# Cross-attention tails as alternating 64x32 tiles, and a new order at the seam to the next stage

## The chip, the cores and the metric

The kernel is one program on one NeuronCore of a Trainium2 chip. The metric is the device time of one execution in microseconds, as the median of a few runs. TensorE is called PE in the profile, and PEld its weight loads; VectorE is DVE, ScalarE ACT, GpSimd POOL, and SyncE (SP) issues most of the DMAs.

## The reference

The input x is 16 batches of 64 rows of 512. Three residual blocks follow, each on a layer norm of x: a cross-attention to 1601 context rows of 256, a causal-masked self-attention (16 query heads, 4 key heads), and a mixture of 8 experts with the best two chosen for each row. The change is in the cross-attention and in the first instructions of the self-attention. The core of the cross-attention, with 16 heads of 32:

```python
y_dca, y_main = y[:, -16:, :], y[:, :-16, :]        # 16 and 1585 rows
q = _ln(heads(x @ Wq + bq))
k, v = _ln(heads(y_main @ Wk + bk)), heads(y_main @ Wv + bv)
k_dca, v_dca = _ln(heads(kv_dca[..., 0])), heads(kv_dca[..., 1])   # from y_dca @ Wkv_dca
ctx = softmax(q k^T * SCALE) v + softmax(q k_dca^T * SCALE) v_dca
out = ctx @ Wo + bo
```

So each query has two softmaxes: one over 1585 main keys and one over 16 second keys. Their weighted values are each divided by their own sum, and then added.

## The kernel before, in words

**Tiles.** The 1585 main rows of a batch are CH = 13 chunks of 128 rows; the last one (column LAST = 12, the "tail") has only LM = 49 rows. A turn of the loop handles two batches, and their chunks are "units" 0 to 25. The tails of the two batches are projected together, in one chunk. A chunk is projected by TensorE to keys and values (split_product, L106, in float32r parts), the keys are normalised per head and transposed (L87), and `scores` (L1300) multiplies them with the queries in 64x128 tiles (L1327). ScalarE takes the exponential into `probs` (L1035), with keys on partitions and 16 heads x 64 queries in the columns. `weighted` (L1331) multiplies values and probs: for each head the stationary operand is 128 rows by 32 columns, the moving operand 64 columns, and the output goes to one of four column tiles (32 partitions of PSUM each), in bank O_BANK. VectorE adds up the probs of the units 0 to 11 in `total` (L1197), for the sum below the fraction.

**The tail.** In the tail's probs buffer the 49 main keys and the 16 second keys lie in different halves of the 128 partitions: `TAIL_ROWS, DCA_ROWS = (0, 64), (DCA_ROW, 0)`, with DCA_ROW = 64. So for the first batch of a pair the main keys are on partitions 0 to 48 and the second ones on 64 to 79, for the second batch the other way round. `g.v_last[:, half, n]` holds the values on all 128 partitions, for n = 0 the main ones and for n = 1 the second ones, each with zeros in the other half. `weighted` makes 16 calls for n = 0 into O_BANK and 16 for n = 1 into V_BANK, all over 128 rows. `counts` (L1355) adds the sums of the probs: four calls of 256 columns a time, with the stationary `g.counted` that is 1 on the rows that count. It is called for n = 1, for n = 0, and at last with `total`, for which it first waits for VectorE (semaphore `pa`). An f32 matmul call stands as two records of LDWEIGHTS and two of MATMUL in the trace.

**Order.** Everything is an order written out by hand for each engine, with semaphores between them. The units come in twelve groups a turn, the last of each batch with three units, (10, 11, 12) and (23, 24, 25). In a group TensorE does the projections of the second group ahead, the transposes of the next, then the weighted values of this group's units and the scores of the next one's. Before unit 11 it waits for `ex` and `ve` of unit 11, and before the tail for `ex` of the tail, `ve` of the latest projected chunk (its values pass through V_BANK, which the tail overwrites) and `vd`, the DMA of the second values. After the tail ScalarE copies both banks to `o_sb` (`o_evac`, L1038), and the next batch's projected values wait for that. The last pair of batches has no next one; there `first_product` and `first_rows` already form the output rows of the first two tiles of the next stage, and `first_seed`, `first_norm` their layer norm. `first_seed(1)` (L1064, ScalarE) stands behind the last `o_evac`.

**The seam.** The cross-attention and the self-attention are two blocks with a barrier between them. Each engine starts the self-attention with a list of increments that sets its semaphores to their first values (L1763, L1842, L1976). TensorE's first work is `turn_x(0, 0)` (L1996), transposes that wait for `xn` (VectorE's list) and `cte` (ScalarE's); ScalarE then evacuates them as xT, and `turn_x(0, 1)` waits for that. The q products follow (L2013). VectorE starts with the normalisation of batch 15's cross-attention (L1847 to L1852), GpSimd splits the weights wo (L1752).

Of the kernel before, what the change touches and what calls it, by code (L numbers as in the profile page):

```python
# [22 lines left out]
B, SQ, D = 16, 64, 512  # L23
# [4 lines left out]
KD = D // P  # L28
# [717 lines left out]
def cross_attention(nc, io, g, psum):  # L746
# [3 lines left out]
    with ExitStack() as ctx:  # L750
# [36 lines left out]
        def unit(i, u):  # L787

            i, u = at(i, u, UNITS)
            return i * UNITS + (UNITS + u + 1)  # L790
# [9 lines left out]
        def tail(n):  # L800

            return column(n) == LAST
# [93 lines left out]
        with nc.Block() as block:  # L896
# [69 lines left out]
            def _(act):  # L966
# [102 lines left out]
                def steps(i, room, guarded):  # L1069
                    for group in range(GR):  # L1070
# [7 lines left out]
                        for j in range(3):  # L1078
# [7 lines left out]
                            if j == len(project) - 1:  # L1086
                                seeds(i, project)
                        if group in (5, 11):
                            o_evac(i * 2 + group // 6, i, GROUP[group][-1])
                        if not room and group == GR - 1:  # L1090
                            first_seed(1)

# [180 lines left out]
            def _(pe):  # L1273
# [57 lines left out]
                def weighted(i, u, latest):  # L1331
                    half = u // CH
                    pe.wait_ge(s["ex"], unit(i, u))
                    pe.wait_ge(s["ve"], projected(i, latest if tail(u) else u))
                    if column(u) == 0:
                        pe.wait_ge(s["oe"], i * 2 + (half + 1))
                    if tail(u):
                        pe.wait_ge(s[f"vd{half}"], i * 16 + 16)
                    for n in range(2 if tail(u) else 1):
                        bank = V_BANK if n else O_BANK  # L1340
                        for k in range(KD):
                            for r in range(4):
                                h = k // 2 * 8 + r * 2 + k % 2
                                v = g.v_last[:, half, n, h, :] if tail(u) else g.v[:, (u - half) % VBUFS, h, :]
                                last = pe.matmul(psum[r * HD:(r + 1) * HD, bank, k * SQ:(k + 1) * SQ], v,  # L1345
                                                 probs[:, buf(u), place(h) * SQ:(place(h) + 1) * SQ],
                                                 start=(k == 0 and (column(u) == 0 or n == 1)), stop=tail(u), skip_group_check=True)
                    if tail(u):
                        for n, bank in ((1, V_BANK), (0, O_BANK)):
                            last = counts(bank, g.counted[:, half * 2 + n], probs[:, buf(u), :], n == 1)  # L1350
                        pe.wait_ge(s["pa"], added(i, u - 1))
                        last = counts(O_BANK, g.counted[:, 4], total[:], True)
                    last.then_inc(s["pv"], 1)

                def counts(bank, rows, src, stop):  # L1355
# [320 lines left out]
def self_attention(nc, io, g, psum):  # L1676
# [6 lines left out]
    with ExitStack() as ctx:  # L1683
# [35 lines left out]
        with nc.Block() as block:  # L1719
# [42 lines left out]
            def _(act):  # L1762
                for stage in ("xe", "qe", "ve", "ex", "pe0", "pe1", "cte"):  # L1763
                    act.sem_inc(s[stage], 2)
# [75 lines left out]
            @block.vector  # L1840
            def _(dve):
                for stage in ("ke", "sm", "mx", "sb", "ri", "co", "x2"):  # L1842
                    dve.sem_inc(s[stage], 2)
                for stage in ("tp", "x1", "bs", "ba", "rn1", "rn2", "rs", "xn"):
                    dve.sem_inc(s[stage], 4)

# [128 lines left out]
            def _(pe):  # L1975
                for stage in ("trx", "qp", "kp", "vp", "sp", "pt0", "pt1", "pv", "trc", "op2"):  # L1976
                    pe.sem_inc(s[stage], 2)
                pe.sem_inc(s["op"], 4)

# [109 lines left out]

                turn_x(0, 0)  # L2090
                turn_x(0, 1)

# [495 lines left out]
```

## Time and profile before

| | us |
|---|---|
| median of 3 runs (1406.8 to 1413.03) | 1407.89 |
| the profiled execution's own time | 1407.75 |
| its span, from the first to the last instruction | 1405.9 |

Busy over the span, from the page:

```profile
PE 1314.5 (93%) x16104; PEld 1078.5 (77%) x16104; DVE 990.8 (70%) x1811; ACT 850.2 (60%) x1535; POOL 311.7 (22%) x354
PE   6889999999999999999999999999999799965896
PEclk9989999999999999999999999999999999986999
```

The first line has each engine's busy us, its share and the number of its instructions. The two others cut the span in 40 slices of 35 us: the busy tenths of TensorE, and its granted clock in tenths of 2.4 GHz. The cross-attention fills the slices 3 to 31, the self-attention follows, and the experts come last. The trace's matmuls are pipelined and overlap, so the sum of their times over a stretch says less than the distance from one start to the next.

### The profile page before, as it was taken

The numbers are of one execution on the slowest core, as the hardware profiler recorded it, in microseconds if no ns is written. First come the engines' busy times: TensorE is split into PE (matmuls) and PEld (weight loads), VectorE is DVE, ScalarE is ACT, GpSimd is POOL, SyncE is SP. The second block draws the span as 40 slices with busy tenths as digits, with TensorE's granted clock in tenths as the row PEclk, the third lists the DMA queues.
The fourth block names the chain that finished last, engine by engine and source line by source line (L and its number), as shares of the span: only waits on it lengthen the run. The fifth ranks groups of instructions, "written<-read, shape, count | busy, mean of one in ns | idle before, by whom it ended". The sixth has DMA issues, their size and how long they took to land. (4 is left out here: it accounts for less than half of the span.)

```text
span 1405.9 us, 42510 instructions
## 1 busy us (share of the span) xinstructions
PE 1314.5 (93%) x16104; PEld 1078.5 (77%) x16104; DVE 990.8 (70%) x1811; ACT 850.2 (60%) x1535; POOL 311.7 (22%) x354
## 2 busy tenths in 40 slices
PE   6889999999999999999999999999999799965896
PEld 3468888888888888888888888888877677744785
DVE  7847677776767776776767777776867656665764
ACT  2346776766777676767766767667666333334653
POOL 2312121221212121221212121221211302111465
PEclk9989999999999999999999999999999999986999
DMA  7042110210210120111112110210200100016887
GB/s 267 16 163 75 47 33 17 96 33 17 70 53 24 32 96 17 33 47 66 33 32 78 36 33 17 97 33 17 75 21 2 65 1 32 31 47 211 210 189 136
DMA packets 35098, 91.26 MB, mean 65 GB/s; under 512 B 4039, under 2 KB 7626, under 8 KB 33418
## 3 DMA queue, kind: packets, MB, share of 16 engines
q1 hardware_dynamic: 28064, 72.38, 15.5%
q0 software_dynamic: 6432, 16.32, 5.2%
q8 instruction: 135, 2.21, 0.7%
q14 instruction: 33, 0.27, 0.1%
q10 hardware_dynamic: 434, 0.08, 0.0%
HBM read 71.93 MB, written 36.01 MB: 77 GB/s over the span
## 5 line engine op out<-in xcount | busy, mean ns | idle before, releaser
L1105 POOL TENSOR_TENSOR y_lo<-y_sb,y_hi 128x256 fp32r<-128x256 f32 x190 | 143.1, 753 | 803.1 <-ACT y_hi L984 803.1
L1018 ACT ACTIVATE ksq<-kc 128x512 f32<-128x512 f32 x200 | 126.4, 632 | 230.0 <-DVE kc L1142 226.4
L1142 DVE TENSOR_TENSOR kc<-psum,bk_sb 128x512 f32<-128x512 f32 x200 | 137.6, 688 | 142.4 <-PE psum L106 139.8
L1035 ACT ACTIVATE probs<-psum 128x1024 f32<-128x1024 f32 x208 | 201.0, 1023 | 39.0 <-PE psum L1327 37.7
L1327 PE MATMUL psum<-qbd,k 64*128 64x128 f32 x3328 | 211.9, 278 | 0.1
L1327 PEld LDWEIGHTS psum<-qbd,k 64*128 64x128 f32 x3328 | 193.3, 188 | 14.0 <-issue 6.3
L1197 DVE TENSOR_TENSOR total<-total,probs 128x1024 f32<-128x1024 f32 x160 | 194.1, 1213 | 1.4 <-ACT probs L1035 1.2
L106 PE MATMUL psum<-wk_hi,y_hi 128*128 128x512 f32 x400 | 177.3, 443 | 11.5 <-issue 8.3
L1148 DVE TENSOR_REDUCE kss<-ksq 128x16 f32<-128x512 f32 x200 | 134.1, 670 | 46.2 <-ACT ksq L1018 45.9
L106 PE MATMUL psum<-wv_hi,y_hi 128*128 128x512 f32 x400 | 157.5, 394 | 2.4 <-ACT v_sb L1011 2.4
L997 ACT ACTIVATE k<-psum,cols_sb 128x512 f32<-128x512 f32 x192 | 150.7, 785 | 13.9 <-PE psum L87 13.9
L106 PE MATMUL psum<-wk_hi,y_lo 128*128 128x512 f32 x400 | 157.7, 394 | 0.0
L106 PE MATMUL psum<-wv_hi,y_lo 128*128 128x512 f32 x400 | 157.1, 393 | 0.0
L106 PE MATMUL psum<-wk_lo,y_hi 128*128 128x512 f32 x400 | 156.8, 392 | 0.0
L106 PE MATMUL psum<-wv_lo,y_hi 128*128 128x512 f32 x400 | 156.3, 391 | 0.0
L1166 DVE SCALAR_TENSOR_TENSOR kn<-kc,kr 128x1024 f32<-128x1024 f32 x96 | 125.8, 1311 | 8.7
L87 PE MATMUL psum<-ident_sb,kn 128*128 128x128 f32 x800 | 120.2, 273 | 3.2 <-DVE kn L1166 3.1
L87 PEld LDWEIGHTS psum<-ident_sb,kn 128*128 128x128 f32 x800 | 98.0, 139 | 32.4 <-DVE kn L1166 7.3
L1011 ACT COPY v_sb<-psum 128x512 f32<-128x512 f32 x192 | 112.3, 585 | 3.6 <-PE psum L106 0.3
L1345 PE MATMUL psum<-probs,v_sb 128*32 128x64 f32 x6144 | 105.7, 220 | 0.0
L1345 PEld LDWEIGHTS psum<-probs,v_sb 128*32 128x32 f32 x6144 | 90.2, 110 | 18.3 <-issue 18.3
L106 PEld LDWEIGHTS psum<-wk_hi,y_hi 128*128 128x128 f32 x400 | 75.5, 189 | 33.7 <-issue 13.6
(272 smaller groups left out, 2033.5 us busy)
## 6 DMA issues: line engine op xcount, KB each, us to landing
y_sb<-in_y SPq DMA_DIRECT2D x48, 512.0 KB, 3.6
slots_dram<-in_blank SPq DMA_DIRECT2D x9, 2080.0 KB
expert_raw<-in_experts SPq DMA_DIRECT2D x8, 1024.0 KB, 6.8
x_sb<-slots_dram SPq DMA_DIRECT2D x23, 260.0 KB, 3.1
x_sb<-in_x SPq DMA_DIRECT2D x1, 1536.0 KB, 10.2
wq<-in_wq SPq DMA_DIRECT2D x4, 256.0 KB, 4.3
xa_wo<-in_wo SPq DMA_DIRECT2D x1, 1024.0 KB, 12.1
y_tail<-in_y_tail SPq DMA_DIRECT2D x8, 128.0 KB, 22.0
```

What stands on the lines that cost most here:

```text
L87: last = pe.transpose(bank[:, k * P:(k + 1) * P], src[:, k * P:(k + 1) * P], ident)
L106: last = pe.matmul(bank, lhs, rhs, start=(n == 0), stop=(n == len(todo) - 1))
L997: last = nc.scalar.activation(k32[:, buf(n)], bank, ACT.Identity, scale=g.cols[:, 2:3], bias=g.cols[:, 3:4])
L1018: nc.scalar.activation(sq[:, buf(n)], kc[:, buf(n)], ACT.Square).then_inc(s["ksq"], 1)
L1035: nc.scalar.activation(probs[:, buf(u), :], psum[:, bank:bank + 2, :].rearrange("p a n -> p (a n)"), ACT.Exp, scale=SCALE).then_inc(s["ex" ...
L1105: nc.gpsimd.tensor_tensor(g.y_lo[:, buf(n)], src, g.y_hi[:, buf(n)].bitcast(F32), ALU.subtract).then_inc(s["ylo"], 1)
L1142: nc.vector.tensor_tensor(kc[:, buf(n)], psum[:, K_BANK, :], g.bk[:], ALU.add).then_inc(s["kb"], 1)
L1148: nc.vector.tensor_reduce(ss[:, buf(n)], head_view(sq[:, buf(n)]), AX_X, ALU.add).then_inc(s["krd"], 1)
L1166: nc.vector.scalar_tensor_tensor(out=kn[:, 0:m].rearrange("p m (h d) -> p (m h) d", d=HD), in0=kc[:, 0:m].rearrange("p m (h d) -> p (m h) ...
L1197: nc.vector.tensor_tensor(total[:], total[:], probs[:, buf(u), :], ALU.add).then_inc(s["pa"], 1)
L1327: last = pe.matmul(out[n][a], k32[rows, k_buf(u), n, :], g.qbd[rows, n, :], start=not guarded, stop=True, skip_group_check=True)
L1345: last = pe.matmul(psum[r * HD:(r + 1) * HD, bank, k * SQ:(k + 1) * SQ], v, probs[:, buf(u), place(h) * SQ:(place(h) + 1) * SQ], start=(k ...
```

## The change

Three things change.

1. The tail. `weighted` sends the tail to a new `weighted_tail`. It makes the same 32 calls for the values and 8 for the counts, but over 64 rows each: those of the main keys and those of the second keys in turn, n = 0 and n = 1 after one another for each head. All values come first, then the counts of both; the total's sums stand behind them, as before over 128 rows. The three waits of the tail move ahead of unit 11 (`tail_ready`).
2. The end of the cross-attention. In the last group ScalarE does `first_seed(1)` before the last `o_evac`.
3. The start of the self-attention. ScalarE's and VectorE's lists of increments begin with those that the first transposes wait for; TensorE gives two of its eleven increments before `turn_x(0, 0)` and nine between `turn_x(0, 0)` and `turn_x(0, 1)`.

```diff
@@ ScalarE, cross-attention, end of a group
+                        if not room and group == GR - 1:
+                            first_seed(1)
                         if group in (5, 11):
                             o_evac(i * 2 + group // 6, i, GROUP[group][-1])
-                        if not room and group == GR - 1:
-                            first_seed(1)
@@ TensorE, cross-attention
                 def weighted(i, u, latest):
                     half = u // CH
-                    pe.wait_ge(s["ex"], unit(i, u))
-                    pe.wait_ge(s["ve"], projected(i, latest if tail(u) else u))
+                    if column(u) == LAST - 1:
+                        tail_ready(i, u + 1, latest)
+                    elif not tail(u):
+                        pe.wait_ge(s["ex"], unit(i, u))
+                        pe.wait_ge(s["ve"], projected(i, u))
                     if column(u) == 0:
                         pe.wait_ge(s["oe"], i * 2 + (half + 1))
                     if tail(u):
-                        pe.wait_ge(s[f"vd{half}"], i * 16 + 16)
...
+                        weighted_tail(u, half)
+                        pe.wait_ge(s["pa"], added(i, u - 1))
+                        last = counts(O_BANK, g.counted[:, 4], total[:], True)
+                    else:
...
+                def tail_ready(i, u, latest):
+                    pe.wait_ge(s["ex"], unit(i, u))
+                    pe.wait_ge(s["ve"], projected(i, latest))
+                    pe.wait_ge(s[f"vd{u // CH}"], i * 16 + 16)
+
+                def weighted_tail(u, half):
+                    parts = [(n, slice(first, first + SQ), (O_BANK, V_BANK)[n])
+                             for n, first in enumerate((TAIL_ROWS[half], DCA_ROWS[half]))]
+                    for k in range(KD):
+                        for r in range(4):
+                            h = k // 2 * 8 + r * 2 + k % 2
+                            for n, rows, bank in parts:
+                                pe.matmul(psum[r * HD:(r + 1) * HD, bank, k * SQ:(k + 1) * SQ], g.v_last[rows, half, n, h, :],
+                                          probs[rows, 2, place(h) * SQ:(place(h) + 1) * SQ],
+                                          start=(k == 0 and n == 1), stop=True, skip_group_check=True)
+                    for r in range(4):
+                        for n, rows, bank in parts:
+                            pe.matmul(psum[r * HD:(r + 1) * HD, bank, KD * SQ:2 * KD * SQ], g.counted[rows, half * 2 + n],
+                                      heads_in(probs[rows, 2, :], r), start=False, stop=(n == 1), skip_group_check=True)
@@ ScalarE, self-attention
-                for stage in ("xe", "qe", "ve", "ex", "pe0", "pe1", "cte"):
+                for stage in ("cte", "xe", "pe0", "pe1", "qe", "ve", "ex"):
@@ VectorE, self-attention
+                for stage in ("xn", "tp", "x1", "bs", "ba", "rn1", "rn2", "rs"):
+                    dve.sem_inc(s[stage], 4)
                 for stage in ("ke", "sm", "mx", "sb", "ri", "co", "x2"):
                     dve.sem_inc(s[stage], 2)
-                for stage in ("tp", "x1", "bs", "ba", "rn1", "rn2", "rs", "xn"):
-                    dve.sem_inc(s[stage], 4)
@@ TensorE, self-attention
-                for stage in ("trx", "qp", "kp", "vp", "sp", "pt0", "pt1", "pv", "trc", "op2"):
+                for stage in ("vp", "trx"):
                     pe.sem_inc(s[stage], 2)
-                pe.sem_inc(s["op"], 4)
...
                 turn_x(0, 0)
+                for stage in ("qp", "kp", "sp", "pt0", "pt1", "pv", "trc", "op2"):
+                    pe.sem_inc(s[stage], 2)
+                pe.sem_inc(s["op"], 4)
                 turn_x(0, 1)
```

## Rows read from the trace of the kernel before

**Rows 1.** Stretches: length, busy PE, PEld, DVE, ACT, POOL; clock, DMA share, GB/s.

```profile
109.80:1090.00 980.20, 971.81 (x13694) 812.45 (x13692) 717.23 (x1072) 680.55 (x1207) 190.93 (x239) 1.00 0.13 44
1098.00:1102.00 4.00, 0.00 (x0) 0.00 (x0) 1.02 (x4) 0.64 (x3) 1.13 (x2) 1.00 0.03 5
1102.00:1108.00 6.00, 4.43 (x20) 4.09 (x21) 5.63 (x3) 2.87 (x3) 2.80 (x5) 0.51 0.96 335
1231.80:1235.00 3.20, 1.19 (x34) 0.92 (x33) 3.17 (x5) 1.06 (x1) 0.00 (x0) 1.00 0.02 5
1235.20:1238.50 3.30, 3.30 (x38) 2.97 (x39) 3.16 (x11) 1.85 (x3) 0.00 (x0) 0.50 0.00 0
```

**Rows 2.** Timeline, PE, first tail: start, us, line, what, tile, count.

```profile
153.56 0.60 PE L87 MATMUL psum<-ident_sb,kn 128*128 128x128 f32 x4
154.09 1.10 PE L1345 MATMUL psum<-probs,v_sb 128*32 128x64 f32 x64
155.01 1.08 PE L1345 MATMUL psum<-probs,v_last 128*32 128x64 f32 x64
155.90 1.05 PE L1358 MATMUL psum<-probs,counted 128*32 128x256 f32 x16
156.76 0.61 PE L1358 MATMUL psum<-total,counted 128*32 128x256 f32 x8
157.31 1.94 PE L1327 MATMUL psum<-qbd,k 64*128 64x128 f32 x30
```

**Rows 3.** Timeline, PE, shorter stretches: the last transpose, the last four sum records.

```profile
153.89 0.27 PE L87 MATMUL psum<-ident_sb,kn 128*128 128x128 f32 x1
...
156.98 0.40 PE L1358 MATMUL psum<-total,counted 128*32 128x256 f32 x4
```

**Rows 4.** Timeline, PE, self-attention scores in 64x64 tiles.

```profile
1153.87 1.10 PE L2038 MATMUL psum<-sa_kT,sa_qT 64*64 64x128 f32 x32
```

**Rows 5.** Timeline, weight loads in flight from 154.08 to 154.14 us.

```profile
154.09 0.16 PEld L1345 LDWEIGHTS psum<-probs,v_sb 128*32 128x32 f32 x8 [0.17 <-issue]
```

**Rows 6.** One line's instructions: ns shortest/median/longest, starts, tile.

```profile
L1345 PEld LDWEIGHTS psum<-probs,v_sb x6144: 106/110/110, 100.9 to 1094.6; 128*32 128x32 f32 x199
L1327 PE MATMUL psum<-qbd,k x3328: 272/272/373, 92.0 to 1090.0; 64*128 64x128 f32 x196
```

**Rows 7.** Timeline, ACT and DVE beside the first tail; brackets: idle before, releaser.

```profile
153.76 0.59 ACT L1011 COPY v_sb<-psum 128x512 f32<-128x512 f32 x1
...
154.37 1.21 DVE L1197 TENSOR_TENSOR total<-total,probs 128x1024 f32<-128x1024 f32 x1
...
157.44 1.07 ACT L1043 COPY o_sb<-psum 128x512 f32<-128x512 f32 x2 [1.58 <-PE psum L1358]
```

**Rows 8.** Timeline, ACT and DVE, end of the cross-attention.

```profile
1096.10 0.18 DVE L1243 BATCH_NORM_AGGREGATE sa_mv<-sa_st 128x2 f32<-128x6 f32 x1
1097.17 1.07 ACT L1043 COPY o_sb<-psum 128x512 f32<-128x512 f32 x2 [5.39 <-PE psum L1358]
...
1098.47 0.20 ACT L114 ACTIVATE sa_rseed<-sa_rlog 128x1 f32<-128x1 f32 x1
...
1099.29 0.55 DVE L1250 TENSOR_SCALAR kc<-x_sb,sa_mv,sa_rs 128x512 f32<-128x512 f32 x1
```

**Rows 9.** One line's instructions: the increments of TensorE and VectorE after the barrier.

```profile
L1977 PEldq EVENT_SEMAPHORE  x10: 51/51/51, 1100.9 to 1102.4; - x10
...
L1845 DVEq EVENT_SEMAPHORE  x8: 21/21/21, 1101.5 to 1102.2; - x8
```

**Rows 10.** Timeline, PE, DVE and POOL, start of the self-attention.

```profile
1102.80 1.09 PE L87 MATMUL psum<-ident_sb,kc 128*128 128x128 f32 x4 [5.70 <-DVEq L1845]
1104.66 1.09 PE L87 MATMUL psum<-ident_sb,kc 128*128 128x128 f32 x4 [0.77 <-ACT sa_xT L1778]
...
1106.39 4.53 POOL L1752 TENSOR_TENSOR wo_lo<-xa_wo,wo_hi 128x2048 fp32r<-128x2048 f32 x1 [2.96 <-ACT wo_hi L1811]
1106.41 4.78 DVE L1852 TENSOR_TENSOR ctxT<-o_sb 128x256 f32<-128x256 f32 x1
```

More of the change, by code:

```diff
@@ L1337, in weighted @@
                     if tail(u):
-                        pe.wait_ge(s[f"vd{half}"], i * 16 + 16)
-                    for n in range(2 if tail(u) else 1):
-                        bank = V_BANK if n else O_BANK
+                        weighted_tail(u, half)
+                        pe.wait_ge(s["pa"], added(i, u - 1))
+                        last = counts(O_BANK, g.counted[:, 4], total[:], True)
+                    else:
                         for k in range(KD):
@@ L1343, in weighted @@
                                 h = k // 2 * 8 + r * 2 + k % 2
-                                v = g.v_last[:, half, n, h, :] if tail(u) else g.v[:, (u - half) % VBUFS, h, :]
-                                last = pe.matmul(psum[r * HD:(r + 1) * HD, bank, k * SQ:(k + 1) * SQ], v,
+                                last = pe.matmul(psum[r * HD:(r + 1) * HD, O_BANK, k * SQ:(k + 1) * SQ],
+                                                 g.v[:, (u - half) % VBUFS, h, :],
                                                  probs[:, buf(u), place(h) * SQ:(place(h) + 1) * SQ],
-                                                 start=(k == 0 and (column(u) == 0 or n == 1)), stop=tail(u), skip_group_check=True)
@@ L1348, in weighted @@
[L1348 to L1352, printed above, removed]
-                    last.then_inc(s["pv"], 1)
+                                                 start=(k == 0 and column(u) == 0), stop=False, skip_group_check=True)
```

## The prediction

> **What bounds the kernel now.** I read the table of stretches first, then one batch's tail in order of time, then the seam between the two stages. In the cross-attention loop TensorE is nearly the only limit: from 109.8 to 1090 us it is busy 971.81 of 980.20 us at the full clock, VectorE 717 and ScalarE 681 [rows 1]. What TensorE stops needing there leaves the span almost whole. At the seam it is another chain: TensorE is idle for 5.70 us up to 1102.80 [rows 10], and small work of ScalarE and VectorE, a barrier and a list of increments set the time.
>
> **A tail today.** Units 10 and 11 are 64 records from 154.09 to 155.01, the tail's v_last products 64 records to 155.90 (0.89 us), its counts 16 records to 156.76 (0.86), the total's sums 8 records to 157.31 (0.55); then come scores [rows 2]. An f32 call leaves two records (32 calls, 64 records): 14 ns a record in the products and 54 in the counts. Alone, a 256-column record would need about 0.22 us: a 128-column transpose holds the array 0.11 us (four last 0.60, the last one 0.27 of it [rows 2, 3]), and the second four sum records start 0.22 us after the first four (156.76 and 156.98 [rows 2, 3]). So the four column tiles already run side by side and the array streams without gaps.
>
> **The new tail.** The same 40 calls use 64 rows each, the batch's own values on one half of the rows and the second values on the other. Eight tiles can be in flight instead of four. Does one row half run beside the other? The self-attention scores are 64x64 tiles, two by two: 32 records of 128 columns in 1.10 us [rows 4]; less the last one's 0.27, as 128 columns last [rows 6], that is 0.12 us for each four, the time of one. The loads keep up there. Eight at once are shown nowhere. They need a load and a matmul every 7 ns; after a change of shape eight loads are issued within 0.16 - 0.11 = 0.05 us [rows 5, 6] (0.11 is one load), 7 ns each, which just suffices: 64 x 7 ns = 0.45 us. Half of the present times is 0.445 for v_last and 0.43 for the counts. Gross gain 0.875 us; the bounds are 0 (the halves take turns) and 0.875.
>
> **Two more changes of shape.** A tail went from 128x128 to 128x32 and then to 64x128. Now 128x32 to 64x32 and back come in between. A new shape starts 0.07 us before the modelled end of the last old matmul: 153.89 + 0.27 against 154.09, and 156.98 + 0.40 against 157.31 [rows 2, 3]. Without a change the next group would have started 0.11 and 0.22 us after the last: the changes cost 0.09 and 0.11, the second also a slow first group (373 against 272 ns [rows 6]), 0.21 in all. For the new ones: into 64x32, a 64-column matmul lasts 0.22, so 0.15 after its start less the 0.04 in which the next would have come, 0.11; back, 0.14, since the last eight starts are spread over 0.05; 0.04 for slower first groups. I take 0.29, nearer to the first row because 32 columns are loaded as there; bounds 2 x 0.09 and 2 x 0.21. Net per tail 0.875 - 0.29 = 0.58 us, bounds -0.42 and +0.70.
>
> The Trainium skill speaks against small tiles: TensorEngine Tiling (Array Packing), Instruction Overhead, gives each matmul some 60 cycles, whatever its columns. At 2.4 GHz that is an estimate of 25 ns; 80 records would take 2.0 us against 1.75 now, and a tail would lose. The trace disagrees, with 14 ns a record [rows 2]: such a cost, if there is one, overlaps between tiles.
>
> **The waits moved ahead of unit 11 (LAST - 1).** There TensorE now asks for the tail's exponentials, the latest values' evacuation and the second values. The evacuation is the late one: it ends at 153.76 + 0.59 = 154.35 [rows 7], 0.26 after unit 10 began, and unit 11 is due 0.46 after. Unit 10 hides it; without that cover it would be up to 0.1 us a tail. Behind the wait in TensorE's queue stand unit 11 and the tail, for which ScalarE's o_sb copies wait. The sums need VectorE's last addition, which ends at 154.37 + 1.21 = 155.58 [rows 7]; they would now start near 156.2: no new wait. The o_sb copies wait for TensorE alone (ScalarE idle 1.58 before them [rows 7]) and move with it, as do the next exponentials. Nothing else closes up, so 15 tails give 15 x 0.58 = 8.7 us. The sixteenth does not count: the seam hides it.
>
> **The seam, its end.** ScalarE copies batch 15's sums from 1097.17 for 1.07 us and only then forms the seed for which VectorE was ready at 1096.10 + 0.18 = 1096.28. The seed is there at 1098.67, VectorE ends at 1099.84, 1.17 later [rows 8]. With the seed first, it is there at about 1096.90 (I allow 0.6) and VectorE ends at 1098.07. TensorE is done near 1096.5, the copies run from 1096.93 to 1098.00; moving them behind the seed delays them by 0.4 us that nobody needs. Both ends come together near 1098.07: 1.77 us earlier.
>
> **The seam, its start.** TensorE's increments begin at 1100.9, 0.1 after the barrier, ten of them to 1102.4 and one more, 0.16 us each; VectorE's last (xn) comes at 1102.2 [rows 9], and the first transposes start at 1102.80 [rows 10], 2.0 after the barrier. Now two increments and a wait stand ahead of them, and xn and cte are first in their lists: 0.6. What is late next is TensorE's own queue: nine increments (1.45 us) ahead of turn_x(0, 1), which starts some 2.5 after the barrier, where before it waited for xT until 1104.66, 3.9 after [rows 10]. The q products gain 1.6, with the transposes still at the full clock. VectorE's list is only reordered and its reciprocal keeps its place; but its ctxT step was held for 4.78 us from 1106.41 beside GpSimd's wo_lo (1106.39, 4.53 us) [rows 10], and wo_lo follows xT and wo_hi, so it comes earlier by as much. Bounds of this step: 0 (VectorE sets the pace) and 1.9 (2.0 - 0.6, and twice half of a 1.09 us group). The loads on SP's queue start 1.8 us earlier and nothing here waits for them.
>
> The clock is 1.00 (2.4 GHz) up to 1102 and 0.51 (nearly all at 1.2 GHz) from 1102 to 1108, after 4 us without a matmul [rows 1]. The new idle is 3.1 us, then 0.5 us of transposes, then 1.3 us idle. A stretch with 1.19 of 3.2 us busy was followed by 0.50, too [rows 1], so I expect the fall again. Between 1105.5 and 1108 or a little more it hit dense work, some 3.4 us, of which half is lost. Where it ends may shift by as much again: I take -0.75 us, bounds +1.7 (no fall) and -1.7. Seam: 1.77 + 1.6 - 0.75 = 2.6 us, bounds 0.1 and 5.4.
>
> **The sum.** 8.7 + 2.6 = 11.3. The profiled execution took 1407.75 us (span 1405.9 and 1.85 around it), 0.14 under the median, 1407.89. 1407.89 - 11.3 = 1396.6; I say 1396.5.
>
> **Rivals.**
> (a) The loads of the two row halves take turns. v_last keeps 0.89 and only the counts halve: 0.43 - 0.29 = 0.14 a tail, 2.1 + 2.6 = 4.7 in all, 1403.2. For it: loads come 14 ns apart now, and eight tiles are new. Against it: the 64x64 tiles [rows 4]. The Trainium skill has a rule near it: TensorE: Matmul & The Clock Gate, "Step-by-step: what each phase is for", lets a load's time go with its columns and not with its rows; by itself it says only that no load gets shorter.
> (b) The other side: no more than four matmuls stream at once, whatever the tiles. Both packed shapes of the trace show four and never more [rows 2, 4]. Nothing is won in a tail and the changes of shape are paid: 15 x 0.29 to 15 x 0.42 = 4.4 to 6.3 us, less the seam's 2.6: 1409.7 to 1411.6. It decides from the point where the eight-tile part of a tail, now 1.75 us, takes 1.75 + 0.17 - 0.29 = 1.63 or more (15 x 0.17 is the seam's gain). Against it: halves by rows run as freely there as tiles by columns.
> (c) VectorE's reciprocal and the held ctxT step set the first keys' copies whatever TensorE does: 1.77 remains, less the clock's 0.75: 9.7 in all, 1398.2.
> (d) The clock does not fall at the seam: +1.7 instead of -0.75, 13.8 in all, 1394.1. For it the shorter idle, against it the half-busy stretch.
>
> **Chances.** Forecast 0.50, (c) 0.18, (d) 0.10, (a) 0.11, (b) 0.07, tails at half their gain 0.04. A measurement of this kernel tells about 0.5%, 7 us, from no change: the line is 1400.9. Forecast, (c), (d) and half of the mixed case lie below it: faster 0.80. (a), the rest of that case and part of (b) lie within: 0.16. Slower by over 7 us needs the upper end of (b) and a lost seam: 0.04. The range, 1393.5 to 1403.5, takes in (d), (c) and (a).
>
> **What would show it.** In a tail: v_last's 64 records in 0.45 us and the counts' 16 in 0.43, the sums 2.1 us after unit 10's start instead of 2.67, scores 2.6 after it instead of 3.22. v_last still at 0.89 means (a) or (b), counts at 0.86 (b). At the seam: seed ahead of the copies, transposes 0.6 us after the barrier, the second ones behind nine increments. The forecast fails if the loop outside the tails grows by what the tails give, as it would if another engine paced it.

## The result and the profile after

The changed kernel takes 1400.21 us, the median of 6 runs (1399.86 to 1401.78), against 1408.18 for the kernel before (6 runs, 1406.8 to 1413.03). The ratio is 0.9938, interval 0.9925 to 0.9952. The forecast was 1396.5: right in direction, inside its range, 3.7 us too low. The profiled execution took 1399.86 us with a span of 1398.0, 7.9 less than the span before.

Busy over the span, and the granted clock, from the page after:

```profile
PE 1308.3 (94%) x16104; PEld 1069.2 (76%) x16104; DVE 990.8 (71%) x1811; ACT 851.0 (61%) x1535; POOL 312.4 (22%) x354
...
PEclk9989999999999999999999999999999999976998
```

The first tail on TensorE (timeline: start, us, line, what, tile, count), answering to [rows 2]:

```profile
154.55 1.10 PE L1348 MATMUL psum<-probs,v_sb 128*32 128x64 f32 x64
155.58 0.80 PE L1368 MATMUL psum<-probs,v_last 64*32 64x64 f32 x60
156.16 0.40 PE L1373 MATMUL psum<-probs,counted 64*32 64x256 f32 x1
156.18 0.22 PE L1368 MATMUL psum<-probs,v_last 64*32 64x64 f32 x1
156.18 0.40 PE L1373 MATMUL psum<-probs,counted 64*32 64x256 f32 x1
156.19 0.25 PE L1368 MATMUL psum<-probs,v_last 64*32 64x64 f32 x3
156.24 0.70 PE L1373 MATMUL psum<-probs,counted 64*32 64x256 f32 x14
156.87 0.64 PE L1379 MATMUL psum<-total,counted 128*32 128x256 f32 x8
157.44 2.06 PE L1327 MATMUL psum<-qbd,k 64*128 64x128 f32 x32
```

From unit 10's start, before and after: the tail's values at +0.92 and +1.03, the counts at +1.81 and +1.61, the total's sums at +2.67 and +2.32, the scores at +3.22 and +2.89. So a tail gained 0.33 us. Twelve of the fifteen tails that count are within 0.03 us of +2.89; three are later, by 1.4 us together. In the kernel before two of the fifteen are, by 1.7 together: stalls that stay.

The same timeline, cut off at two points after the values' first start, shows how many had begun, here x32 within 0.265 us and x33 within 0.275:

```profile
155.58 0.46 PE L1368 MATMUL psum<-probs,v_last 64*32 64x64 f32 x32
...
155.58 0.48 PE L1368 MATMUL psum<-probs,v_last 64*32 64x64 f32 x33
```

In fact 32 had begun within 0.24 us, and the 64th began at 0.642.

The end of the cross-attention, ScalarE and VectorE, answering to [rows 8]:

```profile
1092.41 0.30 ACT L112 ACTIVATE sa_rlog<-sa_mv,cols_sb 128x1 f32<-128x1 f32 x1 [4.53 <-DVE sa_mv L1243]
1092.74 0.20 ACT L114 ACTIVATE sa_rseed<-sa_rlog 128x1 f32<-128x1 f32 x1
1092.93 1.07 ACT L1043 COPY o_sb<-psum 128x512 f32<-128x512 f32 x2
...
1093.56 0.55 DVE L1250 TENSOR_SCALAR kc<-x_sb,sa_mv,sa_rs 128x512 f32<-128x512 f32 x1
```

The start of the self-attention on TensorE, then VectorE and GpSimd, answering to [rows 10]:

```profile
1089.91 1.10 PE L1348 MATMUL psum<-probs,v_sb 128*32 128x64 f32 x64
...
1095.63 0.63 PE L87 MATMUL psum<-ident_sb,kc 128*128 128x128 f32 x4 [2.76 <-DVEq L1864]
1097.21 0.92 PE L87 MATMUL psum<-ident_sb,kc 128*128 128x128 f32 x4 [0.95 <-ACT sa_xT L1799]
1097.92 5.12 PE L2033 MATMUL psum<-sa_xT,sa_wq 128*128 128x128 f32 x32
...
1110.12 1.10 PE L2058 MATMUL psum<-sa_kT,sa_qT 64*64 64x128 f32 x32
```

```profile
1098.76 4.53 POOL L1773 TENSOR_TENSOR wo_lo<-xa_wo,wo_hi 128x2048 fp32r<-128x2048 f32 x1 [1.05 <-ACT wo_hi L1832]
1099.96 3.87 DVE L1870 TENSOR_TENSOR o_sb<-o_sb 128x512 f32<-128x512 f32 x1
```

And stretches there (columns as in [rows 1]), first of the kernel before, then after:

```profile
1102.10:1108.85 6.75, 5.28 (x24) 4.94 (x25) 6.48 (x3) 2.87 (x3) 3.55 (x5) 0.50 0.92 327
```

```profile
1097.42:1100.80 3.38, 3.38 (x18) 3.38 (x17) 3.35 (x2) 1.74 (x2) 2.27 (x3) 0.50 0.91 335
1100.84:1110.00 9.16, 9.16 (x84) 9.15 (x82) 6.56 (x10) 2.22 (x6) 6.61 (x5) 1.00 0.24 98
```

Counted from unit 10 of the last batch (1093.82 before, 1089.91 after), the first transposes come at +8.99 and +5.71, the q products at +11.72 and +8.01, the first scores at +24.14 and +20.20. The 7.9 us of the span are: the loop from its first weighted values (unit 0) to the last unit 10, 992.88 to 988.50, 4.38; the seam up to the scores 3.94; 0.05 after them; and 0.47 lost ahead of the loop, which began later (unit 0's values at 101.41, not 100.94). That last part varies from one profiled kernel to the next, between 100.2 and 103.2.

### The profile page after: what moved, and what is told of

The parts are those of the page before. It is cut to its first block and busy times, and to the rows that moved or that the text cites. A ratio compares the mean times of both kernels' runs of the same rounds, so it can differ in the third digit from the quotient of the medians.

```text
span 1398.0 us, 42494 instructions
## 1 busy us (share of the span) xinstructions
PE 1308.3 (94%) x16104; PEld 1069.2 (76%) x16104; DVE 990.8 (71%) x1811; ACT 851.0 (61%) x1535; POOL 312.4 (22%) x354
## 6 DMA issues: line engine op xcount, KB each, us to landing
xa_wo<-in_wo SPq DMA_DIRECT2D x1, 1024.0 KB, 12.1
```

## The experiments

Ten other kernels and the changed one once more ran in three groups, each group with the kernel before on the same chip (medians 1407.24, 1408.08, 1406.88). The ratios are those on record, to the kernel before of the same group; they are not the quotients of the two medians and differ from them by up to 0.0007.

### The two halves of the change

Tail alone: the changed kernel with the seam as it was.

```diff
-                        if not room and group == GR - 1:
-                            first_seed(1)
                         if group in (5, 11):
                             o_evac(i * 2 + group // 6, i, GROUP[group][-1])
+                        if not room and group == GR - 1:
+                            first_seed(1)
...                      and the three lists of increments as before
```

> The change without its seam (order of the seed and of the three lists of increments as before). By the trace of the changed kernel a tail's scores start 2.89 us after unit 10 instead of 3.22: 15 x 0.33 = 5.0 us. Theory S (the two parts are independent and both real): 1408.2 - 5.0 = 1403.2 us, ratio near 0.9965, the seam from unit 10 of the last batch to the first q products 11.4 us, as before. Rival: the seam's gain is what moves everything and the tails' gain is used up elsewhere: under 2 us of gain here.

Measured: 1404.05 us (9 runs), ratio 0.997, 0.9957 to 0.9983. The tails are as in the changed kernel, scores at +2.89 (two are late); the seam as before less the sixteenth tail's gain: scores +23.76.

Seam alone: the kernel before with the two other parts of the change (the inverse edit).

> Only the seam of the change, tails as before. Theory S: 3 to 4 us less than before, 1404.5 us, since from unit 10 of the last batch to the first q products it is 8.0 us instead of 11.7 in the changed kernel (0.3 of this is the tail's). Rival: most of this is the clock's phase (3.4 us at 1.2 GHz in the changed kernel's profile, 6.8 before) and the median moves by 2 us at most.

Measured: 1403.26 us (10 runs), ratio 0.9974, 0.9964 to 0.9983. First transposes +5.81, q products +7.77, scores +20.21: 3.93 us less than before. The two halves are worth 3.2 and 4.0 us by the medians, 7.2 together; the whole change 8.0 beside its own runs of before, and 6.2 when it was run again (below). So they add up as far as the times can tell. By the intervals the tails give 2.4 to 6.1 us and the seam 2.4 to 5.1, so the seam is worth about as much as the tails, where the forecast had 2.6 against 8.7.

### Why a tail gave 0.33 us and not 0.58

The next kernels change only the order or the size of the tail's calls. Two theories had to explain the break after 32 records. "Supply": the loads and matmuls that TensorE has at hand run out after 32 pairs and refill at a slower pace. "Places in flight": only 32 pairs of load and matmul can be under way, so the 33rd waits until the first is done. The forecast's rival (a) said that loads of the two halves take turns.

Halves in turn: all calls of one row half, then all of the other.

```diff
-                    for k in range(KD):
-                        for r in range(4):
-                            h = k // 2 * 8 + r * 2 + k % 2
-                            for n, rows, bank in parts:
+                    for n, rows, bank in parts:
+                        for k in range(KD):
+                            for r in range(4):
+                                h = k // 2 * 8 + r * 2 + k % 2
...                      the counts likewise, but the other half first
```

> The changed kernel, but the 64-row tiles of one row half all come before those of the other half, values and counts, so that no more than four tiles can stream at once; the two changes of shape stay. It prices the changes of shape alone. Theory P: products 0.89 us and counts 0.86 as before the change, plus 0.29 for the changes of shape: scores 3.5 us after unit 10, 0.6 later than in the changed kernel, 15 x 0.6 = 9 us over it, about 1409 us. Rival: the changes of shape are dearer than 0.29, which would explain why a tail won only 0.33 instead of 0.58: then scores come at 3.75 or later, 1413 us.

```profile
154.53 0.96 PE L1368 MATMUL psum<-probs,v_last 64*32 64x64 f32 x62
155.27 0.38 PE L1373 MATMUL psum<-probs,counted 64*32 64x256 f32 x1
155.29 0.23 PE L1368 MATMUL psum<-probs,v_last 64*32 64x64 f32 x2
155.37 0.66 PE L1373 MATMUL psum<-probs,counted 64*32 64x256 f32 x15
155.96 0.64 PE L1379 MATMUL psum<-total,counted 128*32 128x256 f32 x8
156.53 1.94 PE L1327 MATMUL psum<-qbd,k 64*128 64x128 f32 x29
```

Measured: 1401.87 us (5 runs), ratio 0.9965, 0.9952 to 0.9978; scores at +2.98 in most tails (+3.04 in the one shown), only 0.09 us behind the alternating order. My expectation of 0.6 us a tail failed. The program has all values ahead of all counts, yet a count starts (155.27) before the last two values (155.29): TensorE starts matmuls of different tiles out of the program's order. In the changed kernel the rows at 156.16 and 156.18 show the same. It also finds work for the idle half by itself: in the second tail the starts come in fours, some 56 ns apart, up to 0.267 us, as with four tiles, and from 0.274 on others stand between them. The record does not name the half; that these are the second one's, whose first call is the 33rd, is read from that pattern. The Trainium skill (TensorE: Matmul & The Clock Gate, "The mechanism") has matmuls start and end strictly in the program's order, with only loads pulled ahead; for the starts the rows at 155.27 and 155.29 disagree, and the measurement decides.

Counts between: the 8 calls of the counts after the first half of the values.

```diff
-                    for r in range(4):
-                        for n, rows, bank in parts:
...
+                        if k == 1:
+                            for r in range(4):
+                                for n, rows, bank in parts:
+                                    pe.matmul(...                      the counts' call, unchanged
```

> The changed kernel, but the eight count calls stand between the first and the second half of the value calls. In the changed kernel the first 28 value records of a tail start 7 ns apart and the rest 8.4 ns apart with two gaps of 0.03 and 0.06 us. Theory Q (supply): TensorE's queue holds a store of prepared instructions, and once it is empty they come only every 8.4 ns a pair; while the counts stream (0.43 us for 16 records) the queue fills again, so that the second half of the values runs at 7 ns, too: values to sums 1.05 us instead of 1.29, 0.24 less a tail, 3.6 us in all, about 1396.6 us. Rival theory R (the array): eight tiles of 64 columns can't keep 7 ns for long, since loads of a row half and matmuls of the same half get into each other's way; then the second half takes as long as now and the time stays within 1 us of the changed kernel's.

```profile
154.59 0.45 PE L1368 MATMUL psum<-probs,v_last 64*32 64x64 f32 x32
154.85 0.78 PE L1374 MATMUL psum<-probs,counted 64*32 64x256 f32 x16
155.28 0.81 PE L1368 MATMUL psum<-probs,v_last 64*32 64x64 f32 x32
156.02 0.64 PE L1380 MATMUL psum<-total,counted 128*32 128x256 f32 x8
156.59 2.06 PE L1327 MATMUL psum<-qbd,k 64*128 64x128 f32 x32
```

Measured: 1399.89 us (5 runs), ratio 0.9945, 0.9932 to 0.9958. The sums start at +2.32 and the scores at +2.89, as in the changed kernel (the tail shown is 0.15 us late). The counts gave the time in which a supply could refill, yet in the second tail the second half of the values took 0.44 us for 32 records, 14 ns each and not 7: "supply" falls. The 33rd record is now a count, and starts 0.26 us after the first (154.85 against 154.59): the break stands at the place in the queue, whatever the work.

Narrow values: the tail's value products stream 16 columns instead of 64 (the output lacks 48 of 64 queries in that part).

```diff
-                                pe.matmul(psum[r * HD:(r + 1) * HD, bank, k * SQ:(k + 1) * SQ], g.v_last[rows, half, n, h, :],
-                                          probs[rows, 2, place(h) * SQ:(place(h) + 1) * SQ],
+                                pe.matmul(psum[r * HD:(r + 1) * HD, bank, k * SQ:k * SQ + 16], g.v_last[rows, half, n, h, :],
+                                          probs[rows, 2, place(h) * SQ:place(h) * SQ + 16],
```

> The changed kernel with 16 instead of 64 columns in the tail's value calls; the tail's values for the other 48 queries of each batch are left out. One look at the pace. In the changed kernel the 33rd value record of every tail starts 0.267 us after the first and the 64th 0.642 us after it. Theory F (in flight): TensorE holds at most 32 load-and-matmul pairs, so the 33rd can only start when the first is done; a record with 16 columns is done 0.04 us sooner, so the 33rd starts near 0.227 and the last near 0.54. Rival Q' (supply): pairs are handed out every 8.4 ns whatever they do: 0.267 and 0.642 stay. Rival R (the array's eight tiles can't stream 64 columns at 7 ns): only the columns bind, and with a quarter of them the records run at 7 ns throughout: last at 0.44.

The timeline again, cut off 0.22 and 0.235 us after the first start:

```profile
154.40 0.35 PE L1368 MATMUL psum<-probs,v_last 64*32 64x16 f32 x32
...
154.40 0.40 PE L1368 MATMUL psum<-probs,v_last 64*32 64x16 f32 x33
```

Measured: 1398.93 us (one run); the 33rd record starts 0.227 us after the first, not 0.267. In the tail of the changed kernel one record of 256 columns lasts 0.40 us and one of 64 columns 0.22, so 48 columns are worth 0.18 x 48 / 192 = 0.045 us, and the break ends earlier by about that. In both kernels the 33rd starts 0.027 us behind the modelled end of the first record (0.240 and 0.200 us). So the break ends when the first pair is done: "places in flight" is borne out for it, 32 pairs, that is 64 instructions. The Trainium skill (TensorE: Matmul & The Clock Gate, "The mechanism") gives TensorE a 64-deep window; the trace agrees. What comes behind the break stays open. The 64th value starts at 0.551 us here (expected 0.54) and at 0.642 in the changed kernel: 10.4 and 12.1 ns a record on the average. In the changed kernel the 34th starts 0.056 us behind the 33rd, the next ones 16.7 ns apart up to 0.41, as if only one half had work, and from there both halves together start a record each 8.4 ns; this last pace is the same with 16 columns. 32 places of 0.24 us each would allow one each 7.5 ns, so full places alone do not explain it.

Sums first: the total's sums ahead of the tail, with VectorE's last addition one step earlier, so that the values follow the sums and not unit 11.

```diff
                     if tail(u):
-                        weighted_tail(u, half)
                         pe.wait_ge(s["pa"], added(i, u - 1))
-                        last = counts(O_BANK, g.counted[:, 4], total[:], True)
+                        counts(O_BANK, g.counted[:, 4], total[:], False)
+                        last = weighted_tail(u, half)
```

> The changed kernel, but the total's sums stand before the tail (still 128x32, behind unit 11) and not behind it, so that the tail's 64x32 is followed by the scores' 64x128 at once: one change of shape less in a tail. To have the total ready, VectorE adds unit 11 right after the first k_reduce of that group instead of after the second. Theory: a change back costs 0.14 to 0.16 us, so scores come 0.15 sooner, 2.74 after unit 10, 15 x 0.15 = 2.3 us below the changed kernel, near 1398 us. Rival: the sums' 256-column records leave 0.4 us each in flight, so the tail's first ones start later, and the projection that VectorE now serves 0.4 us later delays TensorE: no gain or a loss.

```profile
155.08 0.62 PE L1382 MATMUL psum<-total,counted 128*32 128x256 f32 x8
155.63 0.80 PE L1370 MATMUL psum<-probs,v_last 64*32 64x64 f32 x60
...
156.92 1.83 PE L1329 MATMUL psum<-qbd,k 64*128 64x128 f32 x28
```

Measured: 1400.24 us (5 runs), ratio 0.9949, 0.9937 to 0.9962: no gain over the changed kernel. The scores start 2.76 us after unit 10 (154.16), 0.13 earlier, 1.9 us over 15 tails. But at the seam the slow clock lasted 6.8 us and the first scores there came at +20.74 instead of +20.20, in the loop of the profiled execution the clock fell once for 3.4 us, and its late tails cost 2.3 us, not 1.4. Whether one change of shape less is worth its 0.13 us in the time is therefore not shown. The 33rd value started 0.267 us after the first here too.

Counts alone: only the 8 count calls use the halves, the values stay over 128 rows, first all of the main keys and then all of the second.

```diff
-                                pe.matmul(psum[...], g.v_last[rows, half, n, h, :],
-                                          probs[rows, 2, ...
+                                pe.matmul(psum[...], g.v_last[:, half, n, h, :],
+                                          probs[:, 2, ...
```

> The changed kernel with the tail's 32 value calls back over all 128 rows (first those of the main keys, then those of the second keys); only the 8 calls for the counts use 64 rows in alternating halves. Theory (places in flight): in the changed kernel the counts, with the change of shape behind them, took 0.71 us (2.32 - 1.61) where they took 0.86 before, and the values with the change ahead of them 1.61 - 0.11 less than before: nearly all of a tail's gain is in the values' first 32 records. Values alone in four tiles keep 0.89 us, the change of shape now stands ahead of the counts: counts at +1.9 us after unit 10's start, sums at +2.6, scores at +3.2, so 0.0 to 0.1 us a tail are gained over before, and with the seam's 4.0 the time is 1403 to 1404. Prediction's sizing (counts halve to 0.43, two changes cost 0.29): counts +1.92, sums +2.49, scores +3.08, 0.14 us a tail, 1402. Scores later than +3.3 would mean that the change of shape costs more than the counts give.

```profile
157.26 1.08 PE L1368 MATMUL psum<-probs,v_last 128*32 128x64 f32 x64
158.26 0.66 PE L1373 MATMUL psum<-probs,counted 64*32 64x256 f32 x16
158.85 0.64 PE L1379 MATMUL psum<-total,counted 128*32 128x256 f32 x8
159.42 1.04 PE L1327 MATMUL psum<-qbd,k 64*128 64x128 f32 x13
```

Measured: 1404.15 us (12 runs), ratio 0.9975, 0.9966 to 0.9984. From unit 10's start (156.34) the counts come at +1.92, the sums at +2.51, the scores at +3.09: 0.13 us gained a tail. The time does not confirm it: with the seam's 4.0 and 15 x 0.13 it should be 6 us under the kernel before, and it is 2.7 by the medians. The profile has the first unit 10 2.2 us later than that of before and the low clock in the loop once, so that its loop is no shorter (939.7 us from the first tail's unit 10 to the last's in both). Over all its executions the granted clock is not lower than that of before (0.976 in both), so the rest is open. The prediction's sizing of counts and shape changes, 0.43 - 0.29 = 0.14, is what was measured, and the theory that I set against it (0.0 to 0.1) had it too low; both readings are of the trace. So of the 0.33 us the values gave 0.20, where the forecast had 0.445.

### The seam

Seed first alone, in the kernel before:

```diff
+                        if not room and group == GR - 1:
+                            first_seed(1)
                         if group in (5, 11):
                             o_evac(i * 2 + group // 6, i, GROUP[group][-1])
-                        if not room and group == GR - 1:
-                            first_seed(1)
```

> The kernel before with one edit: the last seed ahead of the last o_sb copies. Theory: VectorE's last instruction and the barrier come 1.4 to 1.8 us sooner, so about 1.6 us less, ratio 0.9989. Rival: the copies, pushed back by the seed, end the block, so under 1 us is won.

```profile
1100.08 0.63 PE L87 MATMUL psum<-ident_sb,kc 128*128 128x128 f32 x4 [3.79 <-DVEq L1845]
1101.47 1.09 PE L87 MATMUL psum<-ident_sb,kc 128*128 128x128 f32 x4 [0.77 <-ACT sa_xT L1778]
```

Measured: 1406.52 us (11 runs), ratio 0.9991, 0.9981 to 1.0. From unit 10 of the last batch (1093.00) the first transposes come at +7.08, 1.91 earlier than before; the q products at +9.35, 2.37 earlier, as the first transposes now run at the full clock (0.63 us, not 1.09); the scores at +21.15, 2.99 earlier. The slow clock lasted 3.4 us. In the time this is 1.6 us by the medians, as expected, and the interval reaches to no gain: the 2.99 us of the one trace are not confirmed by it.

Increments alone, in the kernel before (the third part of the change as the diff ahead shows it):

> The kernel before with the new order of the three lists of increments only. Theory: first transposes 0.6 instead of 2.0 us after the barrier, q products 1.6 to 2 us sooner, 2 us less, ratio 0.9986, and 3.4 us at 1.2 GHz at the seam instead of 6.8, as in the four kernels with both parts. Rival: the shorter slow stretch needs both parts (the shorter idle), and here it stays 6.8: 1.3 us less.

```profile
1104.27 1.09 PE L87 MATMUL psum<-ident_sb,kc 128*128 128x128 f32 x4 [4.25 <-DVEq L1843]
```

Measured: 1409.66 us (the median of 12 runs, one of which took 3254.89 us and is not in the ratio; its cause is not known), ratio 1.0005, 0.9996 to 1.0014: no gain, where 2 us were expected. In the trace the first transposes come at +7.54 (1.45 earlier), the q products at +10.28 (1.44), the scores at +22.33 (1.81 earlier). But unit 10 of the last batch came at 1096.73, 2.9 us later than before: 1.3 before the first unit 10, and 1.6 in the loop, where the clock was once low for 3.4 us near 1028. Such a fall is worth 1.7 us, an estimate: half of its 3.4. Of the twelve profiles beside that of before, six have it and six have not, but near there, in the last turn, TensorE is idle in all thirteen, fall or not: it waits 2.1 to 2.4 us for ScalarE's copy of the values. The other executions have no profile, only a granted clock: 0.9743 on the average of eleven, against 0.9753 for the 23 of the kernel before. That is an estimate of 1.4 us of dense work (0.001 x 1407), most of what the seam gave. Why this kernel should fall more often is open. The two parts of the seam do not add up in the times: alone they give 1.6 and -1.6 us by the medians, together 4.0.

wo_lo later: in the changed kernel GpSimd's wo_lo waits for VectorE's last step of the cross-attention, to test rival (c).

```diff
                 pool.wait_ge(s["woh"], 1)
+                pool.wait_ge(s["last_on"], 1)
                 nc.gpsimd.tensor_tensor(wo_lo[:], wo[:], wo_hi[:].bitcast(F32), ALU.subtract).then_inc(s["wol"], 1)
```

> The changed kernel, but GpSimd's wo_lo also waits for VectorE's ctxT of batch 15, so that VectorE's product of o_sb (3.87 us beside wo_lo) runs undisturbed. Theory (TensorE sets the seam from the q products on): the product takes some 2.2 us or less and ctxT and the first keys' copies come up to 1.6 us earlier, but TensorE's products are dense from the first q product to the scores, so scores stay at +20.2 us after unit 10's start and the time at 1400. Rival (c of the prediction: VectorE sets the pace of the first scores): scores come 1 to 1.6 us earlier, 1398.6 to 1399.2. Other rival: wo_lo now runs beside the keys' copies, holds them by as much and scores move later by 1 us or more: 1401 or more.

```profile
1099.12 0.69 DVE L1871 TENSOR_TENSOR o_sb<-o_sb 128x512 f32<-128x512 f32 x1
1099.85 0.42 DVE L1874 TENSOR_TENSOR ctxT<-o_sb 128x256 f32<-128x256 f32 x1
1100.42 4.53 POOL L1774 TENSOR_TENSOR wo_lo<-xa_wo,wo_hi 128x2048 fp32r<-128x2048 f32 x1 [3.56 <-DVE ctxT L1874]
1103.13 1.19 DVE L1910 COPY sa_kT<-psum 32x128 f32<-32x128 f32 x4 [2.77 <-PE psum L95]
```

Measured: 1400.86 us (6 runs), ratio 0.996, 0.9947 to 0.9973. VectorE's product took 0.69 us instead of 3.87 and the first keys' copies came 1.7 us earlier (at +14.06, not +15.74), yet the scores stayed at +20.20. From the q products to the scores TensorE has no gap (busy 12.42 of 12.42 us); VectorE sets nothing there. The Trainium skill (SBUF — State Buffer, "SBUF: two separate sides") has VectorE and GpSimd lock each other out when VectorE reads two inputs from SBUF beside a GpSimd operation that reads there; the trace agrees, 0.69 against 3.87 us. In the changed kernel the product ends at 1103.83, 0.54 behind wo_lo's end at 1103.29, about the time that it needs alone.

The changed kernel again:

> The changed kernel itself, unchanged, on the same chip as the two others: 1400.2 us, scores of a tail at +2.89, seam as before (q products +8.0, scores +20.2). A slow stretch of 3.4 us near 1020 us of the loop, which four of the profiled runs had and four had not, may be there: if it is in this run, the loop is 1.7 us longer than in the first run of the same kernel, and it belongs to the run and not to the kernel.

Measured: 1400.65 us (5 runs, 1398.59 to 1401.67), ratio 0.9956, 0.9943 to 0.9969. Seam +5.71, +7.76, +20.20; seven of its fifteen tails were late by 0.1 to 1.1 us, 2.6 together, against 1.4 in the first profile. The changed kernel, halves in turn, counts between, sums first and wo_lo later cannot be told apart: their ratios run from 0.9938 to 0.9965, each interval is 0.0026 wide, and the changed kernel alone gave 0.9938 and 0.9956.

## Why the prediction was right, and what it mis-sized

| step | forecast | measured |
|---|---|---|
| counts in halves, with both changes of shape, a tail | 0.14 | 0.13 (counts alone) |
| values in halves, a tail | 0.445 | 0.20 (0.33 - 0.13) |
| fifteen tails | 8.7 | 4.95 |
| seam, up to the q products | 1.77 + 1.6 = 3.37 | 3.71 (11.72 - 8.01) |
| seam, q products to scores (clock) | -0.75 | +0.23 (12.42 - 12.19) |
| all | 11.3 | 7.9 by the spans |

**What bounds the kernel** was read rightly: what TensorE saved in a tail came off the loop, 4.38 us of 4.95. The rest is within what loops vary: those of two kernels with the same old tail, before and seam alone, differ by 1.2 us.

**The term that failed is the one that sized the values.** The prediction put it so: "They need a load and a matmul every 7 ns; after a change of shape eight loads are issued within 0.16 - 0.11 = 0.05 us, 7 ns each, which just suffices: 64 x 7 ns = 0.45 us." The pace held, but only for 32 records, which began within 0.24 us, 7.7 ns apart. Each record lasts 0.22 to 0.24 us, so by then all places are taken, and the 33rd waited until 0.267; the 64th came at 0.642 instead of 0.44. Of these 0.20 us the wait of the 33rd is 0.04. The other 0.16 came behind it, at 12.1 ns a record, and its cause is open (see narrow values). With 14 ns a record, as before, 32 places last for 0.45 us and never bind, which is why [rows 2] could not show the limit. I had taken eight loads as proof for sixty-four. The missing 0.25 us a tail make 15 x 0.25 = 3.75 us. That this is the size of the whole error (3.7) is luck: the seam gave 1.3 more than forecast, the loop kept 0.6 less than its tails gained, and 0.5 was lost ahead of it. The two changes of shape were sized well: +0.11 into 64x32 as worked out (values at +1.03), and 0.13 in the net that the counts alone left. The change back was not measured by itself.

**Rival (a)**, halves that take turns, falls by the 32 values that started in 0.24 us, and rival (b), only four at once, by the same; their prices, 1403.2 and more, were missed for that reason.

**The waits ahead of unit 11** cost nothing: unit 11 was not late in any tail, and values follow at +1.03. The o_sb copies moved with the sums: ScalarE still waits for TensorE alone ahead of them (1.25 us in the trace after).

**The seam's end and start** came as worked out. Seed alone: transposes 1.91 earlier (forecast 1.77). Increments alone: q products 1.44 earlier (forecast 1.6). TensorE's first transposes started 3.40 us after unit 10's last sums began (1095.63 - 1092.23), 0.56 after the barrier (forecast 0.6). The second ones stood behind the nine increments, as worked out (timeline of ScalarE, and the instructions of one line):

```profile
1096.29 0.59 ACT L1799 COPY sa_xT<-psum 128x512 f32<-128x512 f32 x1 [2.28 <-PE psum L87]
...
L2113 PEldq EVENT_SEMAPHORE  x1: 51/51/51, 1096.9 to 1096.9; - x1
```

xT was there at 1096.88, the last increment (L2113) ended at 1097.00 (1096.95 + 0.05), and the transposes started at 1097.21, 0.33 behind xT. In the kernel before, without increments in between, they started 0.15 behind it (1103.93 + 0.58 = 1104.51, and 1104.66). So the increments still held them by about 0.2 us. The bracket of the row at 1097.21 names ScalarE because it tells only whose semaphore TensorE waited for.

**The clock** fell, so rival (d) is out, but it cost less instead of more. Before, it fell ahead of the first transposes (1102.1) and stayed at 1.2 GHz for 6.75 us, over both groups of transposes and 3.3 us of q products. After, it fell at 1097.4, when the first group had run, and stayed 3.38 us. I had let the slow stretch end as late as before; it lasted half as long. All thirteen profiles sort in one way: where the fall comes ahead of the first transposes the clock stays low for 6.8 us (before, tail alone, increments alone, sums first), where it comes behind them for 3.4 (the nine others). That the place of the fall decides is read from these; no run changed it alone.

**Rival (c)**, VectorE as the pace at the seam, is refuted by the kernel with wo_lo later.

**The sixteenth tail** does not count, as the prediction said, but only because of the seed ahead of the copies. With the old order that tail's 0.33 us still counted (+23.76 against +24.14 in the tail alone), with the new one it does not: transposes at +5.71 with short tails, +5.81 with long ones.

## What to carry to other kernels

Doubling the tiles halved the time of a burst only as long as the burst fitted into what the engine holds in flight: compare a record's length with 32 times the pace before trusting a pace read from the first few. Here 32 x 7 ns is 0.22 us, no longer than a record; 32 x 14 ns is 0.45, twice as long. The burst paid here although it changes shape twice, but half of the gain came from handing the next stage its seed and its first signals in the order in which they are waited for, 3.9 us without a change to any work. And run the parts of a change alone: here one was 3.75 us too high and the other 1.3 too low, and the total shows only the difference. A part of 1 to 2 us needs its trace as well as its time: the increments alone and the counts alone gained in the trace what their times do not show.

## What the runs showed of the hardware beyond that

- TensorE holds 32 pairs of load and matmul: the 33rd of a burst starts only when the first is done (0.267 us after its start with 64 columns, 0.227 with 16).
- Matmuls of different tiles start out of the program's order: a count at 155.27 before two values at 155.29, and the order of the calls in a tail hardly matters (0.09 us).
- Eight tiles of 64x32 started 32 matmuls in 0.24 us, 7.7 ns apart, against 14 ns for four of 128x32; the next 32 came 12.1 ns apart on the average, the last of them at 8.4.
- Stalls of 0.1 to 1.9 us stand at a few tails of every profile, mostly the same ones in kernels with the same tail (the eighth and the fifteenth with the new one). Counted over all records of TensorE and its queue (33,887 with the new tail, 33,903 with the old one), every one of them of over 0.1 us in the tails begins within 8 records of a multiple of 256: in the changed kernel at 4099, 15104 and 27903, that is 16 x 256 + 3, 59 x 256 and 109 x 256 - 1. What comes there, and why it costs time only at a few of these places, no run shows.
